# One table instead of two in a two-layer graph network on one core: all gathers of layer 1 ahead of its additions, gathered rows and messages passed through DRAM

## The chip, the cores and the metric

The kernel runs on one core of one Trainium2 chip. The metric is the device time in microseconds (us); for the kernel before it is 2267.06 us, the median of 3 runs.

## The reference, cut to what matters

```python
# x: (100000, 256) fp32; src, dst: (25000,) int32, dst sorted
deg = maximum(segment_sum(ones, dst, 100000), 1.0); deg_isqrt = deg ** -0.5
# layer 0
h = maximum(_layernorm(x), 0.0)
x = x + deg_isqrt * segment_sum((deg_isqrt * h)[dst] * edge_weight[:, None], src)
# layer 1
h = maximum(_layernorm(x), 0.0)
x_i, x_j = h[dst], h[src]
feat = concatenate([x_i, x_j - x_i])              # (25000, 512)
msg = relu(feat @ W1 + b1) @ W2 + b2              # W1 (512, 512), W2 (512, 256)
x = x + segment_sum(msg, dst) / (segment_sum(ones, dst) + 1e-8)
```

Only rows that are an end of an edge change; the rest of the 100,000 rows (102.4 MB) is copied. Layer 1 must read every row as layer 0 left it, before layer 1 adds anything to it.

## The kernel before, in words

The edges are padded to 200 tiles of 128, in NB = 50 batches of W = 4 tiles. A batch of layer 0 needs four gathers (indirect DMAs of 128 rows of 1 KB) and four scatters (indirect DMAs that add 128 rows into the table). A batch of layer 1 needs eight gathers, for both ends of each edge, and four scatters. All gathers and scatters are issued by GpSimd (POOL) and all go through one software queue.

The prep stage and layer 0 copy `x` into a DRAM table `x1_d` (400 pieces of 250 KB on SyncE's queue, eight in flight), and layer 0 adds into `x1_d`. A barrier ends layer 0. Layer 1 gathers from `x1_d`, while SyncE copies the whole of `x1_d` into `out`, again 400 pieces (L889, L894). The scatters of layer 1 go to `out` and may start only when this second copy is done. POOL's program in layer 1 is written out: first the gathers of LEAD1 = 20 batches (L907), where a batch waits until the batch two before it has been normalized, since `ends` has two buffers; then the wait for the copy; then 100 groups, each of two scatters (L919), three of the remaining gathers while there are any, and a wait until the two scatters have landed. The sums to be scattered lie in `e_ring`, a ring of 20 batches in SBUF.

The other engines run one software-pipelined step per batch. TensorE (PE): `mlp_in` (48 matmuls of 512 columns, `ps_h`), `sums` of the batch before (16 matmuls into `ps_s`, L1240), and twice `turn` (transposes of `e_normed`, `ps_t`) and `mlp_out` (24 matmuls each, `ps_m`). ScalarE (ACT): `std_of`, `hid_high`, `norm` of the next batch (`ends` to `e_normed`), `feat_high`, `scale` of the batch before (`ps_s` to `e_ring`), `out_high`, and the load of `dst_row` for two batches on. VectorE (DVE): the low parts, the comparison tables, and `moments_of` for two batches on.

## Time and profile before

| | us |
|---|---|
| median of 3 runs (2262.39 to 2270.36) | 2267.06 |
| the profiled execution, its own time | 2282.08 |
| its span | 2280.2 |
| layer 1 in it, from the first gather | 1007.4 to 2280.2 |
| POOL busy, PE busy (whole span) | 1280.2, 1762.0 |

The profiled execution is 15.0 us above the median. POOL's busy time leaves out about 0.3 us between two of its DMA instructions, and PE's busy time is modelled from pipelined matmuls, so both are read beside the times at which things start.

### The profile page before, as it was taken

What the parts mean: (1) busy time and instruction counts of PE and PEld (TensorE: products, weight loads), DVE (VectorE), ACT (ScalarE), POOL (GpSimd) and SP (SyncE); (2) the same over time, 40 slices, a digit from 0 to 9 for tenths busy, and PEclk for the clock granted to TensorE, in tenths of its full rate; (3) what the DMA queues carried; (4) which work ended last, traced back from release to release, by engine and by line L of the source; (5) the groups of instructions that cost most, each with busy time, mean ns of one, the idle gap of its engine ahead of it and who ended that gap; (6) DMA issues with size and microseconds to landing.
All of it is one profiled execution on the core that took longest, in us unless ns stands there. A gap on an engine that the chain in (4) does not pass through costs nothing.

```text
span 2280.2 us, 46975 instructions
## 1 busy us (share of the span) xinstructions
PE 1762.0 (77%) x14020; PEld 1536.3 (67%) x14020; DVE 1500.0 (66%) x6001; ACT 1033.7 (45%) x2106; POOL 1280.2 (56%) x1024
## 2 busy tenths in 40 slices
PE   7958888776665667207888888999999999999960
PEld 2258778776665657206777777788888888888850
DVE  8979888886666667205555555667777777777730
ACT  0025454443333333105544554566666666666630
POOL 2032222478888888653332222248888888888754
PEclk9989899998888778658998888999999999999985
DMA  8999999466666666458999999225555555555533
GB/s 297 316 297 338 310 338 311 116 109 101 104 103 104 103 103 104 56 140 279 309 299 295 297 295 292 64 65 94 91 95 97 93 96 99 94 92 97 88 44 39
DMA packets 142793, 379.71 MB, mean 167 GB/s; under 512 B 31805, under 2 KB 97352, under 8 KB 129864
## 3 DMA queue, kind: packets, MB, share of 16 engines
q0 software_dynamic: 86400, 131.14, 32.5%
q1 hardware_dynamic: 27452, 208.63, 26.6%
q10 hardware_dynamic: 28912, 39.64, 6.7%
q14 instruction: 20, 0.16, 0.0%
q8 instruction: 9, 0.15, 0.0%
HBM read 325.72 MB, written 259.17 MB: 257 GB/s over the span
## 4 chain that ended last, share of the span: by engine, by line
PE 24%; issue 11%; POOL 10%; ACT 5%; DMA 3%; DVE 2%; another core or an unknown queue 1%; ACTq 0%; DVEq 0%; POOLq 0%
PE ps_h L1213 12%; PE ps_m L1227 7%; POOL table_out L919 5%; POOL ends L907 5%; PE ps_t L1200 2%; ACT e_normed L1111 2%; DMA table_out<-e_ring,e_targets_all 2%; PE ps_s L1240 2%; ACT hid L1125 1%; DMA ends<-x,keys 1%; DVE e_moments L960 1%; ACT feat_hi L1118 1%; ACT e_ring L1143 0%; DVE out_sum L1032 0%
## 5 line engine op out<-in xcount | busy, mean ns | idle before, releaser
L907 POOL DMA_INDIRECT ends<-x,keys x400 | 402.1, 1005 | 437.4 <-ACT e_normed L1111 312.9
L768 PE MATMUL ps_deg<-table,hot 128*128 128x128 bf16 x5600 | 358.1, 225 | 82.9 <-issue 69.4
L768 PEld LDWEIGHTS ps_deg<-table,hot 128*128 128x128 bf16 x5600 | 334.5, 101 | 101.8 <-issue 92.2
L919 POOL DMA_INDIRECT table_out<-e_ring,e_targets_all x200 | 326.6, 1633 | 108.0 <-issue 54.8
L461 POOL DMA_INDIRECT x<-sums_ring,targets_all x200 | 329.6, 1648 | 89.3 <-issue 65.8
L451 POOL DMA_INDIRECT rows<-in_x,row_idx x200 | 207.4, 1037 | 252.2 <-ACT normed L695 198.2
L1213 PE MATMUL ps_h<-feat_hi,w_hi 128*128 128x512 f32 x800 | 321.3, 402 | 8.9 <-ACT hid L1125 6.5
L1213 PE MATMUL ps_h<-feat_lo,w_hi 128*128 128x512 f32 x800 | 318.8, 399 | 0.5 <-issue 0.5
L1213 PE MATMUL ps_h<-feat_hi,w_lo 128*128 128x512 f32 x800 | 318.2, 398 | 0.7 <-issue 0.7
L782 PE MATMUL ps_sum<-msg_hi,same 128*128 128x260 f32 x800 | 153.3, 321 | 158.8 <-issue 151.7
L1227 PE MATMUL ps_m<-w_hi,hid_hi 128*128 128x256 f32 x800 | 243.1, 304 | 15.6 <-issue 8.3
L1227 PE MATMUL ps_m<-w_lo,hid_hi 128*128 128x256 f32 x800 | 233.7, 292 | 13.4 <-issue 13.4
L1027 DVE TENSOR_TENSOR feat_lo<-ps_t,feat_hi 128x512 fp32r<-128x512 f32 x200 | 130.8, 687 | 165.7 <-ACT feat_hi L1118 87.2
L782 PEld LDWEIGHTS ps_sum<-msg_hi,same 128*128 128x128 f32 x800 | 129.4, 223 | 163.9 <-issue 163.9
L1227 PE MATMUL ps_m<-w_hi,hid_lo 128*128 128x256 f32 x800 | 234.3, 293 | 6.0 <-issue 5.9
L1022 DVE TENSOR_TENSOR hid_lo<-hid,hid_hi 128x512 fp32r<-128x512 f32 x200 | 138.6, 693 | 123.6 <-ACT hid_hi L1128 97.3
L1200 PE MATMUL ps_t<-ident,e_normed 128*128 128x128 f32 x800 | 113.0, 284 | 133.2 <-ACT e_normed L1111 92.5
L1111 ACT ACTIVATE e_normed<-ends,e_shift,e_rstd 128x256 f32<-128x256 f32 x400 | 211.1, 587 | 0.5 <-issue 0.5
L1132 ACT ACTIVATE out_hi<-out_sum 128x512 fp32r<-128x512 f32 x100 | 63.2, 632 | 317.5 <-DVE out_sum L1032 265.0
L1213 PEld LDWEIGHTS ps_h<-feat_hi,w_hi 128*128 128x128 f32 x800 | 151.9, 190 | 52.5 <-ACT hid L1125 10.8
L1200 PEld LDWEIGHTS ps_t<-ident,e_normed 128*128 128x128 f32 x800 | 93.1, 146 | 139.2 <-ACT e_normed L1111 93.1
L513 DVE TENSOR_SCALAR hot<-hi_row,hi_ident 128x1024 bf16<-128x1024 f16 x350 | 147.4, 492 | 49.2 <-issue 21.1
(140 smaller groups left out, 3593.6 us busy)
## 6 DMA issues: line engine op xcount, KB each, us to landing
table_out<-x SPq DMA_DIRECT2D x400, 252.0 KB
x<-in_x SPq DMA_DIRECT2D x400, 250.0 KB
hi_row<-hi_rows ACTq DMA_DIRECT2D x50, 256.0 KB
src_row<-src_rows ACTq DMA_DIRECT2D x50, 256.0 KB
dst_row<-dst_rows ACTq DMA_DIRECT2D x50, 256.0 KB
ends<-x,keys POOLq DMA_INDIRECT x400
rows<-in_x,row_idx POOLq DMA_INDIRECT x200
x<-sums_ring,targets_all POOLq DMA_INDIRECT x200
```

What stands on the lines that cost most here:

```text
L451: pool.indirect_dma_start(out=rows[b % 2][:, j, :], out_offset=None, in_=x, in_offset=bass.IndirectOffsetOnAxis(ap=row_idx[:, W * b + j:W ...
L461: pool.indirect_dma_start(out=x1_d, out_offset=bass.IndirectOffsetOnAxis(ap=targets_all[:, b, j:j + 1], axis=0), in_=sums_ring[:, b % RING ...
L513: last = nc.vector.tensor_scalar(hot[:, c, :, :], hi_row[q][:], hi_ident[:, c:c + 1], None, ALU.is_equal)
L768: last = nc.tensor.matmul(ps_deg[q][k][:, j * P:(j + 1) * P], hot[:, c, k, j * P:(j + 1) * P], table[:, c, part, :], start=(c == 0 and par ...
L782: nc.tensor.matmul(ps_sum[a][:, 0:CW], same[:, j, a * P:(a + 1) * P], msg_hi[:, j, :], start=(j == 0), stop=False)
L907: pool.indirect_dma_start(out=ends[b % 2][:, n, :], out_offset=None, in_=x1_d, in_offset=bass.IndirectOffsetOnAxis(ap=keys[:, 1 - end, at: ...
L919: pool.indirect_dma_start(out=out, out_offset=bass.IndirectOffsetOnAxis(ap=e_targets_all[:, b, j:j + 1], axis=0), in_=e_ring[:, b % RING1, ...
L1022: nc.vector.tensor_tensor(hid_lo[:, m, :], hid[m % 2][:], hid_hi[:, m, :].bitcast(fp32), ALU.subtract).then_inc(hid_lo_done, 1)
L1111: last = nc.scalar.activation(e_normed[:, r, :], ends[q][:, r, :], ACT.Relu, bias=e_shift[q][:, r:r + 1], scale=e_rstd[q][:, r:r + 1])
L1200: last = nc.tensor.transpose(ps_t[k % 2][:, j * P:(j + 1) * P], e_normed[:, end * W + j, c * P:(c + 1) * P], ident[:])
L1213: last = nc.tensor.matmul(ps_h[m % 2][:], w[:, k, m * P:(m + 1) * P], f[:, k, :], start=(k == 0 and n == 0), stop=(k == KF - 1 and n == 2))
L1227: last = nc.tensor.matmul(ps_m[g][:, a * D:(a + 1) * D], h[:, m, at:at + P], w[:, m, :], start=(m == 0 and n == 0), stop=(m == KH - 1 and ...
```

## The change

`x1_d` is gone. `x` is copied once, into `out`; layer 0 adds into `out`, layer 1 gathers from `out` and adds into `out`. For that, all 400 gathers of layer 1 stand ahead of its 200 scatters. Since neither the gathered rows nor the sums of all batches fit in SBUF, they pass through two DRAM tensors:

- Batches 0 and 1 are gathered into `ends`. From batch 2 on a gather goes into `stage_rows[b % 2]`; SyncE writes each half (four gathers, 512 KB) to `ends_d` (`spilled`), and ACT loads two halves back into `ends` at the start of its step, for two batches on (`load_ends`).
- `norm` writes in place, into `ends`, and `e_normed` is gone.
- `scale` writes `e_sums[q]`, ACT stores the batch (512 KB) to `sums_d` at the end of the next step (`keep`), and SyncE loads it back into a quarter of the `stage_rows` buffers (`back`, four batches deep) once all spills are done. POOL scatters from there, with the same wait after each group of two scatters.
- Tiles used by layer 0 alone are given free before layer 1. `dst_f`, a copy of the edge targets as fp32, replaces `per_edge` there.
- DW = 2 equals G = 2, so the matmuls of `sums`, `peers` and `after` are the same in number and shape as before.

```diff
-            out_flat = out...; x1_d = nc.dram_tensor("x1", (ROWS, D), fp32).ap()
+    ends_d = nc.dram_tensor("ends_d", (NB, P, 2 * W * D), fp32).ap()
+    sums_d = nc.dram_tensor("sums_d", (NB, P, W * D), fp32).ap()
...
             @block.sync
             def _(sp):
-                for k in range(FLIGHT):
-                    sp.dma_start(out_flat[k], x1_flat[k]).then_inc(bulk_out[k], 16)
-                with sp.Fori(1, ROUNDS) as r:
-                    for k in range(FLIGHT):
-
-                        sp.wait_ge(bulk_out[k], 16 * r)
-                        sp.dma_start(out_flat[bass.ds(FLIGHT * r + k, 1)],
-                                     x1_flat[bass.ds(FLIGHT * r + k, 1)]).then_inc(bulk_out[k], 16)
+                with sp.Fori(0, HALF - 1) as t:
+                    for q in range(2):
+                        for end in range(2):
+                            sp.wait_ge(staged[q][end], 16 * W * (t + 1))
+                            sp.dma_start(ends_d[...], stage_rows[q][...]).then_inc(spilled[q][end], 16)
+                for q in range(2):
+                    for end in range(2):
+                        sp.wait_ge(spilled[q][end], 16 * (HALF - 1))
+                for b in range(NB):
+                    sp.wait_ge(kept[b % 2], 16 * (b // 2 + 1))
+                    if b >= BACK:
+                        sp.wait_ge(back_free, b - BACK + 1)
+                    sp.dma_start(back(b)..., sums_d[b, :, :]).then_inc(back_in[b % BACK], 16)
...
                 def gather(b, n):
-                    if n == 0 and b >= 2:
-                        pool.wait_ge(e_normed_done, b + 1)
+                    if b >= 4 and j == 0:
+                        pool.wait_ge(spilled[b % 2][end], 16 * (b // 2 - 1))
...
-                for b in range(LEAD1):
+                for b in range(NB):
                     for n in range(2 * W):
                         gather(b, n)
-                for k in range(FLIGHT):
-                    pool.wait_ge(bulk_out[k], 16 * ROUNDS)
-                left = 2 * W * (NB - LEAD1)
-                for c in range(GROUPS * NB):
-                    scatter(c // GROUPS, c % GROUPS)
-                    for n in range(min(left, 3 * c), min(left, 3 * (c + 1))):
-                        gather(LEAD1 + n // (2 * W), n % (2 * W))
-                    scatter_end(c // GROUPS, c % GROUPS)
+                for q in range(2):
+                    pool.wait_ge(ends_first[q], 16 * 2 * W)
+                    for end in range(2):
+                        pool.wait_ge(spilled[q][end], 16 * (HALF - 1))
+                for b in range(NB):
+                    for g in range(GROUPS):
+                        scatter(b, g)
+                        scatter_end(b, g)
...
+                def load_ends(b, t, q):
+                    act.wait_ge(turned, KF * (b - 1))
+                    for end in range(2):
+                        act.wait_ge(spilled[q][end], 16 * t)
+                        act.dma_start(ends[q][:, end * W:(end + 1) * W, :]..., ends_d[...]).then_inc(ends_in[q], 16)
+                def keep(b, q):
+                    act.wait_ge(e_scaled, GROUPS * (b + 2))
+                    act.dma_start(sums_d[...], e_sums[q][:]...).then_inc(kept[q], 16)
```

On POOL's queue, where the lead of gathers ended before, a group of layer 1 was two scatters into `table_out` (the tensor `out`) and up to three gathers:

```order
L907 DMA ends<-x,keys 128x256 [waits e_normed_done]
L907 DMA ends<-x,keys 128x256 x7
L919 DMA table_out<-e_ring,e_targets_all 100800x256 [waits bulk_out5,bulk_out6,bulk_out4,bulk_out7,bulk_out3,e_in_ring,bulk_out2,e_target_ready,bulk_out1,bulk_out0]
L919 DMA table_out<-e_ring,e_targets_all 100800x256
L907 DMA ends<-x,keys 128x256 [waits e_normed_done]
L907 DMA ends<-x,keys 128x256 x2
L919 DMA table_out<-e_ring,e_targets_all 100800x256 [waits e_in_ring,e_scattered]
L919 DMA table_out<-e_ring,e_targets_all 100800x256
L907 DMA ends<-x,keys 128x256 x3
```

On the same queue, the last gathers of batch 49 and the first scatters after the change:

```order
L932 DMA stage_rows<-table_out,keys 128x256 [waits spilled10]
L932 DMA stage_rows<-table_out,keys 128x256 x3
L932 DMA stage_rows<-table_out,keys 128x256 [waits spilled11]
L932 DMA stage_rows<-table_out,keys 128x256 x3
L943 DMA table_out<-stage_rows,e_targets_all 100800x256 [waits spilled10,spilled11,ends_first1,back_in0,spilled01,e_target_ready,spilled00,ends_first0]
L943 DMA table_out<-stage_rows,e_targets_all 100800x256
L943 DMA table_out<-stage_rows,e_targets_all 100800x256 [waits e_scattered]
L943 DMA table_out<-stage_rows,e_targets_all 100800x256
L943 DMA table_out<-stage_rows,e_targets_all 100800x256 [waits e_scattered,e_target_ready,back_in1]
```

No gather stands between a group's scatters and the wait for them any more, and the gathers wait for spills, not for `e_normed_done`.

On ACT's queue, from the last `out_hi` of a step to the first `hid` of the next, before the change:

```order
L1132 ACTIVATE out_hi<-out_sum 128x512 [waits b2_added]
L1092 REGISTER_ALU
L1093 ISA [waits dst_row_free]
L1093 DMA dst_row<-dst_rows 128x512
L1101 ACTIVATE e_std<-e_mean_var,eps_col 128x8 [waits e_rstd_done,e_var_done]
L1124 REGISTER_ALU [waits mm1_done]
L1125 ACTIVATE hid<-ps_h,b_col 128x512 [waits hid_lo_done]
```

The same place after it:

```order
L1173 ACTIVATE out_hi<-out_sum 128x512 [waits b2_added]
L1178 DMA sums_d<-e_sums 128x1024 [waits e_scaled]
L1128 DMA dst_row<-dst_rows 128x512 [waits dst_row_free]
L1136 DMA ends<-ends_d 128x1024 [waits spilled00,turned]
L1136 DMA ends<-ends_d 128x1024 [waits spilled01]
L1145 ACTIVATE e_std<-e_mean_var,eps_col 128x8 [waits e_rstd_done,e_var_done]
L1166 ACTIVATE hid<-ps_h,b_col 128x512 [waits hid_lo_done,mm1_done]
```

One DMA issue has become four, all of them ahead of `e_std` and `hid`.

## Rows read from the trace of the kernel before

**Rows 1.** Source line L919, all scatters of layer 1: duration min/median/max ns, first and last start.

```profile
L919 POOL DMA_INDIRECT table_out<-e_ring,e_targets_all x200: 1552/1622/2093, 1502.1 to 2271.3; - x100
```

**Rows 2.** Timeline of POOL at the very end: start, duration, idle before.

```profile
2263.49 1.55 POOL L919 DMA_INDIRECT table_out<-e_ring,e_targets_all  x1 [3.06 <-DMA table_out<-e_ring,e_targets_all]
2265.34 1.55 POOL L919 DMA_INDIRECT table_out<-e_ring,e_targets_all  x1 [0.30 <-issue]
2269.41 1.55 POOL L919 DMA_INDIRECT table_out<-e_ring,e_targets_all  x1 [2.52 <-DMA table_out<-e_ring,e_targets_all]
2271.27 1.55 POOL L919 DMA_INDIRECT table_out<-e_ring,e_targets_all  x1 [0.30 <-issue]
```

**Rows 3.** Timeline of POOL, one group of two scatters and three gathers.

```profile
1572.42 1.68 POOL L919 DMA_INDIRECT table_out<-e_ring,e_targets_all  x1 [0.30 <-issue]
...
1580.72 1.62 POOL L919 DMA_INDIRECT table_out<-e_ring,e_targets_all  x1 [0.30 <-issue]
```

**Rows 4.** Timeline of POOL during the second copy, the first two gathers of a batch.

```profile
1300.20 0.94 POOL L907 DMA_INDIRECT ends<-x,keys  x1 [17.70 <-ACT e_normed L1111]
1301.45 0.95 POOL L907 DMA_INDIRECT ends<-x,keys  x1 [0.30 <-issue]
```

**Rows 5.** Source line L907, window 1000:1500, what POOL waited for: us, times.

```profile
L907 POOL DMA_INDIRECT ends<-x,keys x159: 940/946/1407, 1007.4 to 1499.6; - x159
  ACT e_normed L1111: 297.2, 18
```

**Rows 6.** Source line L1240 on PE, windows 1075:1440, 1430:1530 and 1550:2165.

```profile
L1240 PE MATMUL ps_s<-out_hi,peers x104: 278/280/281, 1078.6 to 1413.8; 128*128 128x256 f32 x104
...
L1240 PE MATMUL ps_s<-out_hi,peers x32: 278/280/281, 1442.9 to 1518.7; 128*128 128x256 f32 x32
...
L1240 PE MATMUL ps_s<-out_hi,peers x232: 278/280/281, 1558.7 to 2150.4; 128*128 128x256 f32 x116
```

**Rows 7.** Windows: length, busy PE PEld DVE ACT POOL, PEclk, DMA share, GB/s.

```profile
1444.00:1454.00 10.00, 8.01 (x65) 7.58 (x64) 3.29 (x7) 2.25 (x5) 6.62 (x7) 1.00 0.36 105
1560.00:2150.00 590.00, 579.72 (x3585) 510.38 (x3584) 433.01 (x1425) 387.56 (x755) 476.37 (x374) 1.00 0.52 95
2206.00:2275.00 69.00, 0.00 (x0) 0.00 (x0) 0.00 (x0) 0.00 (x0) 34.16 (x22) 0.50 0.39 43
1020.00:1420.00 400.00, 322.64 (x1760) 281.38 (x1760) 215.34 (x728) 198.34 (x378) 119.21 (x125) 0.87 0.91 296
```

**Rows 8.** DMA queues of the whole span: packets, MB, share of 16 engines.

```profile
q0 software_dynamic: 86400, 131.14, 32.5%
q1 hardware_dynamic: 27452, 208.63, 26.6%
q10 hardware_dynamic: 28912, 39.64, 6.7%
```

**Rows 9.** Timeline of the SyncE queue at the start of the second copy.

```profile
1006.62 5.10 SPq L889 DMA_DIRECT2D table_out<-x  x8
...
1012.14 12.78 SPq L894 DMA_DIRECT2D table_out<-x  x8
```

**Rows 10.** Chain that ended last, window 950:1035, landing of batch 0's last gather.

```profile
1016.31 7.96 DMA ends<-x,keys
```

**Rows 11.** Timeline of POOL in layer 0: a batch's last scatter, and the next scatter.

```profile
880.50 1.55 POOL L461 DMA_INDIRECT x<-sums_ring,targets_all  x1 [0.30 <-issue]
...
885.14 1.62 POOL L461 DMA_INDIRECT x<-sums_ring,targets_all  x1 [0.47 <-issue]
```

**Rows 12.** Timeline of ACT: at a step's boundary, and before a step's last `hid`.

```profile
1719.31 0.34 ACTq L1093 DMA_DIRECT2D dst_row<-dst_rows  x1
1720.39 0.67 ACT L1125 ACTIVATE hid<-ps_h,b_col 128x512 f32<-128x512 f32 x1
...
1328.35 0.69 ACT L1125 ACTIVATE hid<-ps_h,b_col 128x512 f32<-128x512 f32 x1 [0.46 <-PE ps_h L1213]
```

**Rows 13.** Timeline of PE during the second copy, a pause inside one step.

```profile
1311.98 1.11 PE L1200 MATMUL ps_t<-ident,e_normed 128*128 128x128 f32 x4 [4.03 <-issue]
```

More of the change, by code:

```diff
@@ L814, in gnn_preln_two_layers @@
             e_shift = [sb(f"e_shift{q}", [P, 2 * W], fp32) for q in range(2)]
-            e_normed = sb("e_normed", [P, 2 * W, D], fp32)
+            stage_rows = [sb(f"stage_rows{q}", [P, 2 * W, D], fp32) for q in range(2)]
             feat_hi = sb("feat_hi", [P, KF, W * P], fp32r)
@@ L841, in gnn_preln_two_layers @@
             ps_s = [pb(f"ps_s{h}", [P, G * D], fp32) for h in range(2)]
+            ends_first = [sem(f"ends_first{q}") for q in range(2)]
             ends_in = [sem(f"ends_in{q}") for q in range(2)]
+            staged = [[sem(f"staged{q}{end}") for end in range(2)] for q in range(2)]
+            spilled = [[sem(f"spilled{q}{end}") for end in range(2)] for q in range(2)]
             dst_row_in = [sem(f"dst_row_in{q}") for q in range(2)]
@@ L871, in gnn_preln_two_layers @@
             e_summed = sem("e_summed")
-            e_in_ring = sem("e_in_ring")
-            e_ring_free = sem("e_ring_free")
+            e_scaled = sem("e_scaled")
+            kept = [sem(f"kept{q}") for q in range(2)]
+            back_in = [sem(f"back_in{k}") for k in range(BACK)]
+            back_free = sem("back_free")
             e_scattered = sem("e_scattered")
@@ L877, in gnn_preln_two_layers, with back @@
             block = stage.enter_context(nc.Block())
+            def back(b):
+                k = b % BACK
+                return stage_rows[k // 2][:, k % 2 * W:(k % 2 + 1) * W, :]
             def following(b, t, q):
@@ L947, in _ @@
                 dve.sem_inc(dst_row_free, 2)
+                nc.vector.tensor_copy(dst_f[:], keys[:, 1, :].rearrange("p (b j) -> p b j", j=W))
                 nc.vector.memset(after[:], 0.0).then_inc(after_made, 1)
                 dve.wait_ge(after_made, 1)
-                nc.vector.memset(after[:, 0, P:G * P], 1.0)
-                nc.vector.tensor_copy(after[:, 0, 0:P], later[:])
-                nc.vector.tensor_copy(after[:, 1, P:G * P], later[:]).then_inc(after_made, 1)
+                for a in range(DW):
+                    if a + 1 < DW:
+                        nc.vector.memset(after[:, a, (a + 1) * P:DW * P], 1.0)
+                    last = nc.vector.tensor_copy(after[:, a, a * P:(a + 1) * P], later[:])
+                last.then_inc(after_made, 1)
                 dve.wait_ge(after_made, 2)
                 def moments_of(b, t, q, part):
-                    if part == 0:
-                        dve.wait_ge(ends_in[q], 16 * 2 * W * (t + 1))
+                    if part == 0 and isinstance(b, int) and b < 2:
+                        dve.wait_ge(ends_first[q], 16 * 2 * W)
+                    elif part == 0:
+                        dve.wait_ge(ends_in[q], 32 * t)
                     for r in range(part * W, (part + 1) * W):
@@ L1054, in step @@
                         feat_low(b + 1, 1)
-                    if second:
+                    if second and not first(b):
                         moments_of(b + 2, t + 1, q, 0)
@@ L1061, in step @@
                     out_low(b, 0)
-                    if second:
+                    if second and not first(b):
                         moments_of(b + 2, t + 1, q, 1)
                     add_b2(b, 1)
-                    if second:
+                    if second and not first(b):
                         mean_var_of(b + 2, t + 1, q)
                     out_low(b, 1)
+                    if second and first(b):
+                        moments_of(b + 2, t + 1, q, 0)
+                        moments_of(b + 2, t + 1, q, 1)
+                        mean_var_of(b + 2, t + 1, q)
                 for b in range(2):
@@ L1106, in norm @@
                         act.wait_ge(e_shift_done, b + 1)
-                        if not first(b):
-                            act.wait_ge(turned, KF * b)
                     for r in range(r0, r1):
-                        last = nc.scalar.activation(e_normed[:, r, :], ends[q][:, r, :], ACT.Relu,
+                        last = nc.scalar.activation(ends[q][:, r, :], ends[q][:, r, :], ACT.Relu,
                                                     bias=e_shift[q][:, r:r + 1], scale=e_rstd[q][:, r:r + 1])
@@ L1165, in step @@
                         if not first(b):
-                            scale(b - 1, 1 - q, g)
+                            scale(b - 1, t - 1 + q, 1 - q, g)
                         out_high(b, g)
+                    if load and first(b):
+                        load_ends(b + 2, t + 1, q)
+                    if not first(b):
+                        keep(b - 1, 1 - q)
                     if load:
@@ L1184, in _ @@
                 for g in range(GROUPS):
-                    scale(NB - 1, 1, g)
+                    scale(NB - 1, HALF - 1, 1, g)
+                keep(NB - 1, 1)
             @block.tensor
@@ L1200, in turn @@
                         last = nc.tensor.transpose(ps_t[k % 2][:, j * P:(j + 1) * P],
-                                                   e_normed[:, end * W + j, c * P:(c + 1) * P], ident[:])
+                                                   ends[q][:, end * W + j, c * P:(c + 1) * P], ident[:])
                     last.then_inc(turned, 1)
```

131 lines of the change are left out of this document (73 added, 58 removed).

## The prediction, made before the changed kernel ran

> **What bounds the kernel now.** I read the source line of the layer 1 scatters first. Its last instruction starts at 2271.3 us and the span ends at 2280.2 [rows 1], so POOL's chain sets the end. Layer 1 occupies POOL from 1007.4 [rows 5], and it splits in three. In the lead (1007.4 to 1502.1 [rows 1, 5]) POOL is not the limit: it issues a gather every 1.25 us (1300.20 to 1301.45 [rows 4]), so its 159 gathers need 199 us, and it waits 297.2 us, 18 times, for `e_normed` [rows 5]. It is PE that paces the lead: from the first start of `ps_s` to the last, less 1.6 us inside one step, 13 steps take (1413.8 - 1.6 - 1078.6) / 12 = 27.8 us each [rows 6]. In the second part a group of two scatters and three gathers takes 1580.72 - 1572.42 = 8.3 us [rows 3], and POOL hardly waits: busy 476.37 of 590 us [rows 7], the rest mostly the 0.30 us between instructions. PE steps take (2150.4 - 1.6 - 1558.7) / 28 = 21.1 us there [rows 6]. In the third part only scatters are left: a group pair takes 2269.41 - 2263.49 = 5.92 and, by the idle times 2.5 and 3.1 that alternate, 6.5 us [rows 2], so about 6.25 per group. As a check: the 240 gathers left make 80 groups with gathers and 20 without, and (2271.3 - 1502.1 - 20 x 6.25) / 80 = 8.05 [rows 1]. The wait in it is for the landing of its own second scatter. PE has two steps and its last `sums` to go at 2150.4 [rows 6], so it is done near 2200 and POOL trails it by some 80 us at the end.
>
> The second copy holds layer 1 in two ways: no scatter may start before it ends, and while it runs the DMA share is 0.91 [rows 7] and PE pauses inside its steps, as the 4.03 us ahead of four transposes that wait for nothing the trace shows [rows 13]. Between the end of the copy and the mixed part, with bursts of gathers but no copy, a step still takes (1518.7 - 1.6 - 1442.9) / 3 = 24.7 us [rows 6].
>
> **The change part by part, POOL's chain.** Prep and layer 0 keep their instructions; only the name of the table they add into changes. I cost that at nothing, so the first gather starts at 1007.4.
>
> *Gathers.* 400 at 1.25 us are 500 us, 10.0 per batch, if nothing holds them. What can hold them is the spill. A half of `stage_rows` is four gathers; the next gather into it starts 13 gathers, 16.25 us, after the half's last gather was issued. In that time the gather must land (3.8 to 8.0 us: below, the scatter pair's landing, 5.92 - 1.85 = 4.1 less waking [rows 2]; above, the first batch under the copy [rows 10]), SyncE must issue (0.64 us, 5.10 / 8 [rows 9]), and 512 KB must land in DRAM. The trace has no such store; the nearest row is the first 250 KB piece of the copy, waited for at 1012.14 and issued from 1006.62, so 5.5 us [rows 9]; I take 5 to 8. The sum is 9.5 to 16.7 us: usually inside 16.25, so 10.0 per batch is the lower bound and a little more is likely.
>
> *The DMA engines.* Eight gathers in 10 us alone have share 0.36 [rows 7], 0.45 us of all 16 engines each. One scatter has 0.39 x 69 / 22 = 1.22 us [rows 7]. For 512 KB on a hardware queue: 208.63 MB took 0.266 x 2280 = 606 us, so 1.5 us; by q10 (39.64 MB, 6.7%) 2.0 us [rows 8]; I take 1.7. The gather phase then needs per 10 us 3.6 + 2 x 1.7 = 7.0 us, and per 21 us PE step two loads, one `keep` and a `dst_row`, 3 x 1.7 + 1.0 = 6.1. That is 0.70 + 0.29 = 0.99, or 0.91 by 1.5 us. It is near full. Against a collapse speaks that under the copy, with share 0.91, POOL still issued at 1.25 us [rows 4]. I take 10.3 us per batch.
>
> *Turnover.* After the last gather (landing, spill, first `back`) I add 15 us: 4 + 5.5 + 5.5.
>
> *Scatters.* 100 groups with nothing between the second scatter and the wait: 6.25 us each alone, 12.5 per batch. New beside them are the loads, `keep` and `back`, 2.8 transfers of 512 KB per 12.5 us, a share of about 0.4 beside scatter's own 0.4. The trace prices this once: in layer 0, with 0.5 MB per batch of other loads (a share of about 0.1), a batch's last scatter had landed 885.14 - 880.50 = 4.6 us after its start [rows 11]; this is one of 18 such places between 480 and 900 us, which range from 4.6 to 5.6 with mean 4.95, against 1.55 + 3.06 = 4.6 with nothing beside it [rows 2]; 0.25 to 0.3 us for 0.1 of share. Scaled to 0.3 to 0.4 of share this is 0.6 to 1.0 us per group, less since `back` is issued just after a landing and falls in the first scatter's shadow. I take 13.7 per batch. Bounds: 12.5 (all hidden), and 12.5 + 2.8 x 1.7 = 17.3 (none hidden).
>
> The Trainium skill, "DMA: Bandwidth & Descriptors", section "Issuing engines are not separate DMA queues", says that DMAs of all issuing engines run on the same 16 DMA engines and interleave. This speaks against the change: by it none of the new traffic is free. If each queue had engines of its own the scatters would keep 12.5 us per batch and the sum below would be 60 us less; the 4.95 against 4.6 us above agrees with the page.
>
> *Sum.* 1007.4 + 50 x 10.3 + 15 + 50 x 13.7 = 2222, and 4.5 us from the last wait to the end of the span (8.9 [rows 1] less the 4.4 that the last group's period holds): a span of 2227, own time 2229.
>
> **PE's chain, which must not be longer.** The first `ps_s` stays at about 1078.6. Until 1537 the gather bursts go on; I take the 24.7 us of the stretch with bursts and no copy (bounds 21.1 and 27.8 [rows 6]): 19 steps, to 1548. After that 29 steps at 21.1 + 0.6. The 0.6 is ACT: three more DMA issues of 0.34 us and their address registers, some 1.5 us, ahead of `hid`, which starts 1.1 us after the `dst_row` issue now [rows 12]. Its cover is ACT's idle time before the last `hid`, 0.46 us [rows 12], and about 0.4 us between `hid_lo` and `mlp_out`; without cover it is 1.5. That gives 2177, and 11 us for the last step, 2188. The tail is new: `scale` 2, store 5, load 5, two groups 6.25 + 7 = 25 us. PE's chain ends at 2213, 14 us before POOL's. In-place `norm`, `dst_f` and the smaller tiles are costed at nothing: same shapes, on DVE and ACT under PE's 21 us. The wait of `load_ends` for `turned` and `spilled` ahead of `e_std` and `hid` on ACT is long met: the spills run at 10 us per batch against PE's 21 or more; only at batch 2 may a few us be lost, and the first landing without the copy (4 instead of 8 us) gives them back.
>
> The profiled execution lies 15 us above the median, so **the median should be 2229 - 15 = 2214 us**.
>
> **The rivals.**
> 1. *All transfers hide.* 10.0 and 12.5 us per batch: 1007.4 + 500 + 15 + 625 + 4.5 = 2152, median 2139. For it: small packets, and POOL kept its pace under a busier copy. Against: the 4.95 against 4.6 us. Chance 0.15.
> 2. *PE is the bound.* Its pauses under DMA load stay as under the copy, 27.8 us for 16 steps (to 1523), and ACT's 1.3 us come in full, 32 steps of 22.4: 2240, and 11 + 25: 2276, median 2262, level with before; with 21.7 us steps 2240. For it: the share in the gather phase is as high as under the copy. Against: pieces of 4 KB, not 16 KB, and no wait that explains the pauses. Chance 0.13.
> 3. *Slower: the DMA queues hold POOL.* The mechanism is the landing of spills, then of scatters. The point from which it decides: (2280.2 - 1007.4 - 15 - 4.5) / 50 = 25.1 us for the two together, against my 24.0, so only 1.1 us per batch away. Spills that land after 19 instead of 16 us make 11.5 per batch (two batches share the excess), and a `back` or load behind each second scatter 15.0: 26.5, span 2352, median 2336. For it: the share of 0.99 and the bound of 17.3. Chance 0.18.
> That removing the copy does nothing is excluded: POOL's 297 us of waits in the lead [rows 5] hang on it.
>
> **How the numbers follow.** My forecast has 0.54, its own range 2180 to 2255. With rival 1 below and part of rivals 2 and 3 above, 8 in 10 lie between 2140 and 2300. Under 0.3% (7 us) a change cannot be told from none: faster is below 2260. Faster: 0.54 + 0.15 + half of rival 2, 0.75; same 0.07; slower 0.18.
>
> **What would show it.** The last gather of layer 1 should start near 1520, with short waits for the SyncE spill at every fourth gather; the first scatter near 1537; groups of 6.6 to 7.0 us, with waits of 3 to 4 us for their own landing; PE steps of 24 to 25 us before 1540 and 21.5 to 22 after; POOL's last scatter some 10 to 15 us later than PE's own chain would give. The prediction is wrong if a gather batch takes over 11 us or under 10, if groups take over 7.5 us, or if POOL waits for `back` (PE bound) over a long stretch.

## The result

The changed kernel takes 2630.91 us (median of 4, 2629.06 to 2632.29) beside 2268.71 us for the kernel before: ratio 1.159, interval 1.1543 to 1.1637. The forecast was 2214 us, faster, with a range of 2140 to 2300: the sign is wrong, and the range ends 330 us below the result.

Each set of runs was made in one session on a chip, and the sessions came in two kinds: in one ("held") the kernel before takes 2264 to 2277 us and the changed one 2630, in the other ("free") 2152 to 2162 and 2283. The result above, and the trace ahead of the prediction, are from held sessions.

The page's slices of the changed kernel, and its costliest groups:

```profile
PE   7788878766656611111102139999999999999994
DVE  9888889776766711000000027777777777777772
POOL 2132234888888856777777723332333232233333
PEclk9899999888887856555555559999999999999997
DMA  8999995665656544666666635555555555555554
...
L943 POOL DMA_INDIRECT table_out<-stage_rows,e_targets_all x200 | 326.1, 1630 | 760.4 <-DMA stage_rows<-sums_d 533.5
L932 POOL DMA_INDIRECT stage_rows<-table_out,keys x384 | 392.0, 1021 | 121.4 <-issue 121.4
```

Each digit is 66 us. While POOL gathers (from the sixteenth digit to the twenty-fourth), PE is mostly at 0 to 2 tenths; before, PE was busy for 0.81 of the lead (322.64 of 400 [rows 7]). Only after the gathers does PE run, and then it is full to the end, so POOL's scatters wait 533.5 us for `back`, that is for PE. The source lines of POOL date it (gathers, then scatters):

```profile
L932 POOL DMA_INDIRECT stage_rows<-table_out,keys x384: 945/950/1929, 1020.9 to 1532.8; - x192
L932 POOL DMA_INDIRECT ends<-table_out,keys x16: 945/949/1023, 1000.7 to 1019.6; - x16
  issue: 125.9, 399
...
L943 POOL DMA_INDIRECT table_out<-stage_rows,e_targets_all x200: 1552/1567/2068, 1577.7 to 2618.8; - x100
  DMA stage_rows<-sums_d: 533.5, 46
  DMA table_out<-stage_rows,e_targets_all: 128.6, 51
  DVE e_targets_all L1049: 65.6, 3
```

POOL did what was forecast: 400 gathers from 1000.7 to 1532.8 us, 10.66 us per batch, and no wait for the spill. PE did not. Its `ps_s` line, windows 1010:1560 and 1560:2627:

```profile
L1298 PE MATMUL ps_s<-out_hi,peers x8: 275/326/418, 1425.1 to 1438.0; 128*128 128x256 f32 x8
...
L1298 PE MATMUL ps_s<-out_hi,peers x392: 274/282/387, 1576.4 to 2593.1; 128*128 128x256 f32 x196
```

These rows set against [rows 6] are the whole result. Eight matmuls of this form are one batch. Before, 13 batches were done by 1413.8 us. Now one is done by 1560, and the other 49 begin at 1576.4. All but the last follow each other at the usual pace: the last batch's come 11 us behind the one before, so (2593.1 - 11 - 1576.4) / 47 = 21.4 us is a step, and 1576 + 47 x 21.4 = 2582, with 45 us of last step and tail, is the span of 2627. What PE does meanwhile is this (timeline of PE, then of POOL, at 1200 us):

```profile
1202.09 0.37 PE L1283 MATMUL ps_m<-w_lo,hid_hi 128*128 128x256 f32 x1 [1.73 <-issue]
1204.88 0.37 PE L1283 MATMUL ps_m<-w_hi,hid_lo 128*128 128x256 f32 x1 [2.43 <-issue]
1207.68 0.37 PE L1283 MATMUL ps_m<-w_hi,hid_hi 128*128 128x256 f32 x1 [2.43 <-issue]
1210.48 0.37 PE L1283 MATMUL ps_m<-w_lo,hid_hi 128*128 128x256 f32 x1 [2.43 <-issue]
...
1200.97 0.95 POOL L932 DMA_INDIRECT stage_rows<-table_out,keys  x1 [0.30 <-issue]
1202.22 0.95 POOL L932 DMA_INDIRECT stage_rows<-table_out,keys  x1 [0.30 <-issue]
```

One matmul starts every 2.80 us and waits for nothing that the trace names ("issue"). ACT sees the same beat (timeline of ACT): each of the four slices of `hid` needs 12 matmuls, and 12 x 2.80 = 33.6 us lie between two of them, while ACT's own instructions keep their length.

```profile
1071.91 0.69 ACT L1166 ACTIVATE hid<-ps_h,b_col 128x512 f32<-128x512 f32 x1 [32.13 <-issue]
...
1105.50 0.69 ACT L1166 ACTIVATE hid<-ps_h,b_col 128x512 f32<-128x512 f32 x1 [30.77 <-remote]
...
1139.10 0.69 ACT L1166 ACTIVATE hid<-ps_h,b_col 128x512 f32<-128x512 f32 x1 [30.77 <-remote]
```

The two views agree in the total and not in the detail. PE's own records of the 12 matmuls ahead of the middle one stand close together (timeline of PE, first and last of the 12, then the next slice):

```profile
1072.65 0.80 PE L1269 MATMUL ps_h<-feat_hi,w_hi 128*128 128x512 f32 x1 [27.23 <-ACT hid L1166]
...
1077.45 0.40 PE L1269 MATMUL ps_h<-feat_hi,w_lo 128*128 128x512 f32 x1
1106.24 0.80 PE L1269 MATMUL ps_h<-feat_hi,w_hi 128*128 128x512 f32 x1 [28.39 <-ACT hid L1166]
```

By these records the slice is done near 1078, yet ACT, which waits for it, starts at 1105.50. The profile models the ends of matmuls, so for the 512-column matmuls the 2.80 us is worked out from ACT's rows. Over the whole gather phase it is 500 us for 215 matmuls, 2.3 us each.

PE's granted clock falls to the 1.2 GHz level in this stretch (0.5 in the slices), after PE has stood mostly idle: a 256-column matmul then takes 0.37 us, and that explains nothing of the 2.8.

Loading of code is not it either, as far as the trace records it: in the window 1200:1350 PE has 48 matmuls, and these two are all the DMA queues that moved anything, neither of the kind "instruction":

```profile
q0 software_dynamic: 5301, 14.48, 37.9%
q1 hardware_dynamic: 4132, 15.03, 26.8%
```

### The profile page after: what moved, and what is told of

Same layout as the page of the kernel before. It is cut to its first block, busy times and chain, and to the rows that moved or that the text cites. A ratio compares the mean times of both kernels' runs of the same rounds, so it can differ in the third digit from the quotient of the medians.

```text
span 2627.3 us, 45849 instructions
## 1 busy us (share of the span) xinstructions
PE 1776.8 (68%) x14020; PEld 1532.8 (58%) x14020; DVE 1493.3 (57%) x6002; ACT 1028.4 (39%) x2106; POOL 1286.3 (49%) x1024
## 3 DMA queue, kind: packets, MB, share of 16 engines
q10 hardware_dynamic: 49936, 116.19, 14.9%
## 4 chain that ended last, share of the span: by engine, by line
another core or an unknown queue 16%; ACT 15%; issue 10%; DVE 8%; PE 8%; ACTq 3%; DMA 1%; POOL 1%; DVEq 0%; POOLq 0%
ACT ends L1152 8%; PE ps_m L1283 6%; ACT hid L1166 4%; DVE out_sum L1063 2%; DVE e_moments L991 2%; ACTq L1136 2%; DVE feat_lo L1058 1%; ACT hid_hi L1169 1%; PE ps_h L1269 1%; DVE hid_lo L1053 1%; ACT feat_hi L1159 1%; DVE out_lo L1068 1%; ACTq L1178 1%; ACTq L1128 1%
## 5 line engine op out<-in xcount | busy, mean ns | idle before, releaser
L943 POOL DMA_INDIRECT table_out<-stage_rows,e_targets_all x200 | 326.1, 1630 | 760.4 <-DMA stage_rows<-sums_d 533.5
L932 POOL DMA_INDIRECT stage_rows<-table_out,keys x384 | 392.0, 1021 | 121.4 <-issue 121.4
L1269 PE MATMUL ps_h<-feat_hi,w_hi 128*128 128x512 f32 x800 | 328.2, 410 | 169.2 <-ACT hid L1166 142.7
L464 POOL DMA_INDIRECT table_out<-sums_ring,targets_all x200 | 330.8, 1654 | 87.9 <-issue 63.9
L1283 PE MATMUL ps_m<-w_hi,hid_hi 128*128 128x256 f32 x800 | 236.5, 296 | 106.9 <-DVE hid_lo L1053 72.2
L1283 PE MATMUL ps_m<-w_hi,hid_lo 128*128 128x256 f32 x800 | 227.3, 284 | 32.4 <-issue 32.2
L1166 ACT ACTIVATE hid<-ps_h,b_col 128x512 f32<-128x512 f32 x200 | 133.9, 670 | 245.9 <-remote 207.7
L1256 PE MATMUL ps_t<-ident,ends 128*128 128x128 f32 x800 | 110.5, 282 | 173.5 <-ACT ends L1152 85.7
L1283 PEld LDWEIGHTS ps_m<-w_hi,hid_hi 128*128 128x128 f32 x800 | 154.3, 193 | 119.8 <-DVE hid_lo L1053 84.4
L1152 ACT ACTIVATE ends<-ends,e_shift,e_rstd 128x256 f32<-128x256 f32 x400 | 211.1, 588 | 0.5 <-DVE e_shift L1006 0.5
```

The costliest lines, as they stand in the source:

```text
L464: pool.indirect_dma_start(out=out, out_offset=bass.IndirectOffsetOnAxis(ap=targets_all[:, b, j:j + 1], axis=0), in_=sums_ring[:, b % RING0 ...
L932: pool.indirect_dma_start(out=(ends if b < 2 else stage_rows)[b % 2][:, n, :], out_offset=None, in_=out, in_offset=bass.IndirectOffsetOnAx ...
L943: pool.indirect_dma_start(out=out, out_offset=bass.IndirectOffsetOnAxis(ap=e_targets_all[:, b, j:j + 1], axis=0), in_=back(b)[:, j, :], in ...
L1152: last = nc.scalar.activation(ends[q][:, r, :], ends[q][:, r, :], ACT.Relu, bias=e_shift[q][:, r:r + 1], scale=e_rstd[q][:, r:r + 1])
L1166: nc.scalar.activation(hid[m % 2][:], ps_h[m % 2][:], ACT.Relu, bias=b1_col[:, m:m + 1])\
L1269: last = nc.tensor.matmul(ps_h[m % 2][:], w[:, k, m * P:(m + 1) * P], f[:, k, :], start=(k == 0 and n == 0), stop=(k == KF - 1 and n == 2))
```

## The experiments

At first sight three things are new beside PE in that stretch: gathers without a pause, the spills, and the loads that ACT issues. The theory was that the unbroken gathers hold PE by themselves; the rivals were the DMA traffic of spills and loads, and, for the kernel before, its second copy.

**Session 1, free** (before 2152.42 us), each kernel run once. The first kernel takes the second copy out of the kernel before; all but one of its 400 pieces are left out, so most output rows are unwritten.

```
             def _(sp):
-                for k in range(FLIGHT):
-                    sp.dma_start(out_flat[k], x1_flat[k]).then_inc(bulk_out[k], 16)
...
+                sp.dma_start(out_flat[0], x1_flat[0]).then_inc(bulk_out[0], 16)
```

> The kernel before, with one piece of the second copy in place of 400 (it leaves the rest of the output rows unwritten; everything else as before). Theory B (bursts): PE is held by streams of gathers that POOL issues without a pause, whatever else the DMA engines do; then a PE step of the lead, with its burst of 8 gathers, stays at 25 us or more (27.8 with the copy), and the whole is 2220 to 2275 us. Theory S (share): PE is held because the DMA engines are full (share 0.91 under the copy); then a lead step falls to about 21.1 us, POOL's first scatter comes near 1385, and the whole is 2150 to 2175 us.

Measured: 2151.88 us. Its lead steps are 20.4 to 20.5 us with 8 gathers in a burst. It equals the kernel before of its session, which was itself 116 us faster than in the result. So the question could not be tested there. PE was not held in this kernel, and by its time not in the kernel before either (no trace of that one from a free session was kept).

The second kernel lets POOL wait, in the changed kernel, for the landing of every 4 gathers.

```
                         .then_inc(ends_first[b] if b < 2 else staged[b % 2][end], 16)
+                    if j == W - 1 and b >= 2:
+                        pool.wait_ge(staged[b % 2][end], 16 * W * (b // 2))
```

> The changed kernel, in which POOL waits after every 4 gathers until they have landed (from batch 2 on). Theory B: pauses of about 4 us free PE, so PE steps in the gather phase take 21 to 27 us instead of about 190; a batch of gathers takes about 18 us, the last starts near 1900, and POOL's 100 groups at 6.25 follow: 2540 to 2600 us in all. Theory S: the share falls from 0.65 to about 0.4, with the same result; only if neither holds does PE stay frozen and the whole exceed 2900 us.

Measured: 2544.03 us. POOL waits 356.9 us, 95 times, and PE's steps during the gathers are 21.1 to 22.1 us.

The third keeps the gathers but drops the spills: ACT loads rows of `x` in place of the gathered rows, so layer 1 computes on other data.

```
-                            sp.wait_ge(staged[q][end], 16 * W * (t + 1))
-                            sp.dma_start(ends_d[bass.ds(2 * t + 2 + q, 1), :, end * W * D:(end + 1) * W * D]
...
-                                      ends_d[bass.ds(b, 1), :, end * W * D:(end + 1) * W * D]
+                                      x_chunks[bass.ds(b, 1), :, end * W * D:(end + 1) * W * D]
```

> The changed kernel without the spills: SyncE writes nothing to ends_d, POOL waits for the landing two batches back instead, and ACT loads its rows from x (so layer 1 computes on other rows; sizes, counts and places of all other work are unchanged). Theory B: the gathers alone freeze PE; PE matmuls of the gather phase still start about 2.8 us apart, the gather phase takes about 500 us, and the whole is 2580 to 2630 us. Theory S: with a third or so of the traffic gone (share under 0.5) PE steps of the gather phase fall to 21 to 25 us and the whole to 2150 to 2230 us.

Measured: 2276.59 us, between the two ranges expected, with PE's steps 21.4 us and POOL waiting 346.8 us for the landing of its own scatters. I could have read this as proof that the spills hold PE. It was not: the changed kernel itself takes 2283 in such a session.

The fourth spaces the gathers with an iota of 1024 columns.

```
+                    if b >= 2:
+                        pool.wait_ge(padded_n, 2 * W * (b - 2) + n)
+                        nc.gpsimd.iota(pad_i[:], [[1, PADW]], base=0, channel_multiplier=0).then_inc(padded_n, 1)
```

> The changed kernel with a POOL instruction of about 1.2 us (an iota into a scratch tile) after every gather from batch 2 on; POOL stays busy and waits for no landing, gathers come every 2.6 to 2.8 us. Theory B in its strict form (only a pause for landings frees PE): PE stays frozen for some 1050 us, the whole is over 3000 us. Theory R (the rate of gathers decides, 0.8 per us holds PE and 0.37 per us, as in the mixed part of the kernel before, does not): PE steps of 21 to 27 us in the gather phase, and the whole is about 2700 us, set by POOL.

Measured: 2559.43 us where about 2700 was expected, since a gather came every 2.2 us and not every 2.6 to 2.8; PE steps of 23 to 28 us during the gathers, 21.5 after.

**Session 2, held** (before 2269.26 us), runs repeated: both kernels unchanged.

> The changed kernel as it is. The kernel before took 2152.4 us on the chip of the first experiments and 2268.7 us where the change was timed, so both need a trace from one chip. If the freeze of PE under the gathers belongs to the changed program: about 2630 us again. If it belongs to the chip or the placement of that execution: PE steps of 21 to 27 us in the gather phase, and 2150 to 2280 us.

> The kernel before as it is, on the same chip. Where it takes about 2152 us its PE steps under the second copy should be 20.5 to 22 us and its chain at the end POOL's or PE's alike; where it takes about 2268 us they should be 27.8 us.

Measured: 2631.47 us, ratio 1.1598 (1.1574 to 1.1621), and 2271.44 us, ratio 1.0011 (0.9989 to 1.0034). The result repeats, with the idle PE and the lead steps of 27 to 31 us.

**Session 3, free** (before 2159.98 us), on another chip, each kernel run once: three kernels of session 1 again, and the changed kernel beside them.

> The changed kernel as it is, as the yardstick of this group, since the two groups so far ran on different chips (before: 2152 on one, 2269 us on the other). Theory C (chip): where before takes about 2152 us, PE is not frozen under the gathers and this takes 2200 to 2290 us; where before takes about 2269, it takes 2630. Theory P (program: the streams of gathers together with the spills freeze PE on any chip): 2630 on either.

> The changed kernel without spills, its rows read from x (as e3). On a chip with before at 2269: theory G (the gathers alone freeze PE there) says matmuls of the gather phase about 2.8 us apart and 2600 to 2630 us; theory P says PE runs free and 2230 to 2290 us. On a chip with before at 2152: 2277 again.

> The kernel before with one piece of the second copy (as e1; most output rows stay unwritten). On a chip with before at 2269: theory G says a lead step with its burst of 8 gathers stays over 24 us, 2230 to 2269 us; theory P says 20.5 us and about 2152. On a chip with before at 2152: 2152 again.

> The changed kernel with a wait for the landing after every 4 gathers (as e2). On a chip with before at 2269: if pauses of about 4 us free PE, steps of 21 to 27 us in the gather phase and 2540 to 2560 us; if bursts of 4 already hold PE, steps over 30 us and over 2700. On a chip with before at 2152: 2544 again.

Measured: 2282.60, 2262.58, 2152.52 and 2535.04 us. The first is the most useful trace of the study, for here the changed kernel runs as forecast in kind. Its POOL source lines, and then two windows, of its gather and its scatter phase (length, busy PE PEld DVE ACT POOL, PEclk, DMA share, GB/s):

```profile
L932 POOL DMA_INDIRECT stage_rows<-table_out,keys x384: 942/946/1425, 1024.6 to 1515.9; - x192
L932 POOL DMA_INDIRECT ends<-table_out,keys x16: 942/946/1022, 1004.5 to 1023.3; - x16
...
L943 POOL DMA_INDIRECT table_out<-stage_rows,e_targets_all x200: 1552/1566/2045, 1528.6 to 2272.2; - x100
  DMA table_out<-stage_rows,e_targets_all: 365.3, 95
  DMA stage_rows<-sums_d: 11.7, 1
```

```profile
1010.00:1510.00 500.00, 455.77 (x2732) 394.96 (x2733) 337.89 (x1123) 301.38 (x587) 381.17 (x391) 0.97 0.85 276
1560.00:2100.00 540.00, 526.83 (x3226) 458.83 (x3225) 381.86 (x1275) 346.01 (x676) 218.89 (x137) 1.00 0.66 149
```

The same window of the changed kernel in the held session of the result:

```profile
1010.00:1510.00 500.00, 76.35 (x215) 54.82 (x216) 32.48 (x116) 29.27 (x53) 381.38 (x376) 0.53 0.64 199
```

POOL is equally busy in both (381 us). PE has 2732 matmuls in one and 215 in the other, and the DMA share is higher where PE runs. A full DMA is therefore not what stops PE.

**Session 4, held** (before 2263.64 us), runs repeated: no spill, and the wait after 4.

> The changed kernel without spills (as e3 and e8), wanted on a chip where before takes about 2269 us and the changed kernel 2630. Theory G (there the stream of gathers alone holds PE): matmuls of the gather phase about 2.8 us apart, 2600 to 2630 us. Theory P (gathers and spills together are needed): PE steps of 21 to 25 us, 2230 to 2290 us. On a chip of the other kind: 2263 to 2277 us as before, and nothing new.

> The changed kernel with a wait for the landing after every 4 gathers (as e2 and e10), wanted on the same kind of chip. If pauses of about 4 us free PE: steps of 21 to 27 us in the gather phase and 2535 to 2560 us, some 80 us faster than the changed kernel there. If bursts of 4 already hold PE: steps over 30 us, over 2700 us. On a chip of the other kind: 2535 to 2544 us.

Measured: 2626.32 us, ratio 1.1611 (1.1558 to 1.1664), and 2527.28, ratio 1.1173 (1.1107 to 1.1239), 8 us under the range expected. The windows of the gather phase, of the kernel without spills and then of that with the waits:

```profile
1010.00:1510.00 500.00, 73.89 (x216) 52.88 (x217) 32.47 (x116) 29.25 (x53) 381.03 (x376) 0.53 0.35 103
```

```profile
1010.00:1510.00 500.00, 464.33 (x2777) 402.31 (x2778) 338.49 (x1134) 307.10 (x597) 232.63 (x239) 0.97 0.62 202
```

Without spills the DMA share is 0.35 and PE is held all the same, 216 matmuls for 215. With a pause of 348.7 / 95 = 3.7 us after every 4 gathers PE is free, at a share of 0.62. These two runs separate the theories: the gathers hold PE, and a pause frees it. The time stays long because POOL pays for the pauses, and its last gather starts at 1826.6 us.

**Session 5, held** (before 2276.97 us), on a fourth chip, runs repeated but for the last kernel.

> The kernel before without its second copy (one piece of it is kept, so most rows of the output stay unwritten). If POOL's bursts of 8 gathers hold TensorE by themselves, the lead's steps stay at 27 to 28 us and the time at 2245 to 2270 us. If it takes the copy beside them, the steps fall to 20.5 us, as they did in the first such run, and the time to about 2152.

Measured: 2203.63 us, ratio 0.9669 (0.9627 to 0.971). Neither end of the expectation: the lead's steps are 21.7 to 24.7 us, mean (1444 - 1070) / 16 = 23.4. A burst of 8 alone costs some 3 us per step, and with the copy beside it about 7. So the copy does deepen the hold in the kernel before, which the theory in its plain form did not say.

> The changed kernel with an iota of 1024 columns after each gather of layer 1, beside kernels whose TensorE stands still under the gathers. The gathers then take until about 1876 us (2.25 us each, instead of 1.33). If what holds TensorE is how close the gathers follow each other, its steps are 23 to 27 us meanwhile and the time is that of the first run, 2550 to 2570. If it is that POOL never pauses for a landing, TensorE still stands until 1876, and 48 steps of 21.5 us and the tail give about 2950.

Measured: 2565.72 us, ratio 1.1257, last gather at 1857.5, PE steps of 23 to 27 us, as in the free session. POOL never pauses for a landing here, and PE is not held. So what counts is not the missing wait as such, but how many gathers follow each other how closely.

Nor are the 2 to 5 us by which these steps exceed 21.5 a rest of the hold: they are there in the free session too, where the changed kernel's steps are 21.4 to 22.3 but for two, and the trace gives them another cause. These are PE's costliest wait and two VectorE lines in window 1100:1500 of this run, then the same VectorE lines of the changed kernel in the free session, and last this run's window 1010:1510:

```profile
L1289 PE MATMUL ps_m<-w_hi,hid_hi 128*128 128x256 f32 x268 | 85.5, 319 | 44.3 <-DVE hid_lo L1059 44.3
L1026 DVE TENSOR_SCALAR peers<-dst_row,dst_col 128x256 fp32r<-128x256 f32 x64 | 57.3, 955 | 0.2
L1059 DVE TENSOR_TENSOR hid_lo<-hid,hid_hi 128x512 fp32r<-128x512 f32 x65 | 54.7, 841 | 13.4 <-ACT hid_hi L1175 13.4
...
L1053 DVE TENSOR_TENSOR hid_lo<-hid,hid_hi 128x512 fp32r<-128x512 f32 x72 | 49.9, 693 | 35.7 <-ACT hid_hi L1169 35.6
L1020 DVE TENSOR_SCALAR peers<-dst_row,dst_col 128x256 fp32r<-128x256 f32 x72 | 23.5, 386 | 0.5
...
1010.00:1510.00 500.00, 428.67 (x2466) 375.23 (x2467) 358.31 (x1012) 271.61 (x529) 458.25 (x457) 0.93 0.60 188
```

Beside the iotas VectorE's comparison takes 955 ns for 386 and `hid_lo` 841 for 693, and PE waits for `hid_lo`, not for "issue". POOL is busier here (458 us of 500) than in the changed kernel (381), so a busy POOL is not what holds PE.

The third kernel turns the finding to use. It is the kernel **before**, with one wait in the lead:

```
                         .then_inc(ends_in[b % 2], 16)
+                    if b < LEAD1 and n == W - 1:
+                        pool.wait_ge(ends_in[b % 2], 16 * (2 * W * (b // 2) + W))
```

> The kernel before, with POOL waiting in the lead for the landing of each batch's first 4 gathers before it issues the other 4. POOL has 297 us to spare there. If unbroken gathers hold TensorE and a pause of about 4 us frees it, some 16 steps of the lead fall from 27.8 to 21 to 22 us, and the time from 2265 to 2155 to 2180, below both kernels. If the lead's long steps come from the second copy's traffic, nothing changes: 2260 to 2275.

Measured: 2181.23 us (2180.41 to 2188.73), ratio 0.9581 (0.9548 to 0.9615). It beats both kernels in a held session. The source lines of its gathers in the lead and of `ps_s` in window 1075:1440, then its window 1010:1410:

```profile
L907 POOL DMA_INDIRECT ends<-x,keys x160: 940/946/1461, 1004.2 to 1409.8; - x160
  ACT e_normed L1113: 107.8, 17
  DMA ends<-x,keys: 102.0, 20
...
L1242 PE MATMUL ps_s<-out_hi,peers x138: 278/280/281, 1080.2 to 1439.7; 128*128 128x256 f32 x138
```

```profile
1010.00:1410.00 400.00, 359.62 (x2189) 315.29 (x2190) 267.40 (x896) 241.36 (x467) 154.53 (x156) 0.95 0.94 318
```

POOL waits 102.0 us for landings and 107.8 for `e_normed`, where it waited 297.2 [rows 5]; together that is less, because the steps it waits for fall from 27.8 to 21.1 us. The lead ends at 1409.8 instead of 1499.6 [rows 5], and those 90 us are nearly all of the gain. The second copy is still there, and moves at 318 GB/s for all traffic instead of 296 [rows 7]. So the copy, which the change removes as the culprit, deepens the hold (the first kernel of session 5), but the lead gets its short steps back with the copy in place.

> The changed kernel once more, one look with no timed rounds, in one session with timed ones. If the two levels seen so far (2630 and 2283 us) belong to the session, it is 2630 us here with the kernel before at about 2265; if they belong to looks without timed rounds, it is about 2283.

Measured: 2630.06 us. A kernel that is run only once can show the held level; the level goes with the session.

**Session 6, free** (before 2161.70 us), on the same chip as session 5, each kernel run once.

> The kernel before with the waits in the lead once more. In a session in which the kernel before takes 2150 to 2160 us, its lead steps are 20.5 us already, so the waits have nothing to give: 2150 to 2185 us. In one in which it takes about 2265, again 2175 to 2195.

> The changed kernel with a pause for the landing after every 8 gathers of layer 1 instead of every 4: 10.3 us of gathers and 3.7 us of pause, so the gathers last until about 1016 + 48 x 14 = 1690 us and POOL's scatters, 6.8 us a group, until about 2370. If a burst of 8 still holds TensorE (some 6 us in each step of the lead of the kernel before), TensorE does 14 to 20 steps by 1690 and ends at 2390 to 2450; if not, POOL decides, at 2350 to 2385.

The second of the two has the wait once per 8 gathers:

```
+                    if n == 2 * W - 1 and b >= 2:
+                        pool.wait_ge(staged[b % 2][end], 16 * W * (b // 2))
```

Measured: 2177.56 us and 2417.26 us. Where PE is not held, the waits in the lead cost 16 us (0.7%, one run of each): POOL now waits 142.3 us for landings. The 2417.26 us lie in the range that was expected of a held PE (2390 to 2450), and yet POOL sets it: its last gather starts at 1693.9, and a group of scatters takes 7.0 us where 6.8 was taken. The wait per 8 leaves PE's steps at 21.3 to 22.3 us, but in a free session that says nothing of a burst of 8 in a held one. That stays untried.

| session | chip | kernel before | changed kernel |
|---|---|---|---|
| of the result | not recorded | 2268.71 | 2630.91 |
| 1 | 2 | 2152.42 | not run |
| 2 | 1 | 2269.26 | 2631.47 |
| 3 | 12 | 2159.98 | 2282.60 |
| 4 | 2 | 2263.64 | not run |
| 5 | 7 | 2276.97 | 2630.06 |
| 6 | 7 | 2161.70 | not run |

Chips 2 and 7 appear in both kinds, so the kind is not the chip's. One thing goes with the kind throughout: in the free sessions (1, 3 and 6) every kernel was run once, and in the held ones (2, 4, 5 and the result's) kernels were run repeatedly. The fourth run of the changed kernel was a single one in a held session and was held, so the repetition of a kernel by itself does not decide; whether that of its neighbours does was not tried. What sets the kind is open. Kernels whose gathers are paused or spaced nearly agree in both: 2181.23 and 2177.56 us with the waits in the lead, 2527.28 (held) and 2544.03 and 2535.04 with the wait after 4, 2565.72 and 2559.43 with the iota.

## Why the prediction was wrong

**The step that failed is PE's chain.** "I take the 24.7 us of the stretch with bursts and no copy (bounds 21.1 and 27.8)": measured, PE does one step in the whole gather phase. Both bounds were read from a lead in which POOL gathers for 10 us and then rests for 17.7. The changed kernel's gathers have no rest, so 27.8 was no upper bound; it was the price at a duty of 10 in 27.8. The rows shown would have told it. The step was 27.8 - 21.1 = 6.7 us longer for 10 us of gathers [rows 6], so PE lost 0.67 of the time that a burst lasts. At a duty of one a step is 21.1 / 0.33 = 64 us, 7 steps fit before 1537, 41 steps of 21.7 are left, and with 11 and 25 us of last step and tail the sum is 2463: PE bound and slower, though still short of the 2627 measured. The rest would need a hold that grows with the length of the burst, which is argued below and not shown. [Rows 13] showed the pause too, 4.03 us on a PE that waits for nothing. I put it down to the second copy's load, because the copy was the other thing running. Session 5 parts the two: the copy deepens the pause, and a wait between gathers removes it with the copy in place. In the free session the same term was off the other way: the steps of the gather phase were 21.4 to 22.3 us but for two (20.8 and 23.7), where 24.7 was taken.

**The copy was not gating the scatters either.** "No scatter may start before it ends" is so in the program, but these windows of the kernel before (columns as in [rows 7]) show that the copy was over first:

```profile
1420.00:1430.00 10.00, 5.26 (x25) 4.87 (x26) 4.61 (x10) 4.09 (x9) 1.70 (x2) 0.57 0.83 272
1430.00:1440.00 10.00, 10.00 (x45) 8.42 (x45) 7.37 (x29) 6.10 (x12) 0.00 (x0) 0.91 0.08 26
```

The traffic ends near 1430, and the first scatter starts at 1502.1 [rows 1], just behind the lead's last gather at 1499.6 [rows 5]. What delayed the scatters was the lead, and so PE.

**Rival 2 had the right bound and the wrong size.** It said PE, and gave 2262 us with 27.8 us steps for 16 steps. The sign that the last section named, POOL waiting for `back` over a long stretch, is what the trace shows (533.5 us).

**POOL's chain was mostly right, and is seen in the free session.** Gathers: 10.3 us per batch forecast, (1515.9 - 1004.5) / 49.9 = 10.25 measured, with a DMA share of 0.85 where 0.99 was feared, and no wait for a spill. Turnover: 15 forecast, 1528.6 - 1515.9 = 12.7. Scatters: 13.7 per batch forecast, (2272.2 - 1528.6) / 49.75 = 14.9 measured; the term is 60 us too small. The wait for a scatter's own landing was 365.3 / 95 = 3.85 us against 3.06 and 2.52 with nothing beside it [rows 2]. I had discounted the scaled price (0.6 to 1.0 us per group) because `back` falls in the first scatter's shadow; no run shows that shadow, and the upper end, 1.0, without a discount gives 14.5, near what was measured. The Trainium skill, "DMA: Bandwidth & Descriptors", section "Issuing engines are not separate DMA queues", had the sign of this term (DMAs of all issuers share the 16 engines); the trace agrees, with 14.9 for 12.5. With 14.9 the sum 2227 becomes 2287, against 2280.7. The kernel without spills is 20 us shorter (2262.58 for 2282.60, one run of each), but its first scatter starts no earlier (1529.7 for 1528.6): the gain lies behind the last spill, where the two differ only in what ACT loads, so it prices no spill, and which of the loads, `keep` and `back` costs the 60 us stays open. The steps after the gathers were 21.4 to 22 us where 21.7 was taken. One figure of the rivals is a slip that changes nothing: a span of 2352 gives a median of 2339 by the rule used for the others, not 2336.

**Even so the change would not have gained.** In the free session POOL sets the end, as forecast, and the changed kernel is still 5.7% slower than the kernel before (2282.60 for 2159.98, one run of each). The forecast gain compared a POOL chain without pauses with a kernel before whose lead was itself held: its 18 waits for `e_normed`, 297.2 us [rows 5], came from steps of 27.8 us; in the free session they are 66.5 us in the kernel before with the waits in its lead, whose steps are 20.4 to 21.6. What the prediction hung on removing the copy was, for the most part, the hold. Taking the copy out gains 0.5 and 7.5 us in the free sessions and 73 in a held one; pausing the gathers of the lead gains 96 there with the copy in.

**What is shown and what is only argued.** Shown: unbroken gathers hold PE without the spills (session 4), a pause of 3.7 us after 4 frees it (sessions 4 and 5), a spacing of (1857.5 - 1021.0) / 383 = 2.18 us instead of 1.33 does so too, though at this spacing the iotas slow VectorE, and the kind of session decides whether any of it happens. Excluded: a full DMA, the spills, a busy POOL, and recorded loading of code. Argued: that the hold grows with the burst. Per step a burst of 4 costs 0 to 1 us, one of 8 some 3, an endless one takes over 90% of PE's work (215 matmuls for 2732 in the same 500 us); something that fills while gathers are in flight and drains in a pause would do this. That is a guess: no view names it, and no run measured it. Open, too, is why the copy adds 4 us per step, and what makes a session held.

## What to carry to other kernels

An interference price read from a trace belongs to the duty at which it was read: divide it by the time of the disturbing work, and scale it to the duty after the change, before calling it a bound. Before merging bursts of indirect gathers into one long run, look for matmuls that start at an even spacing and wait for nothing; where they are there, a wait for a landing after every 4 gathers, on a POOL that has slack, is a two-line change that gained 4.2% in a held session here, and cost 0.7% (one run) in a free one. And run the kernel before in more than one session before believing that what its trace shows is the kernel's.

## What the runs showed of the hardware

- In held sessions, under gathers issued every 1.25 to 1.33 us without a pause, TensorE starts one matmul of 256 columns per 2.80 us, and by ScalarE's rows one of 512 columns takes as long (three slices of `hid` 33.6 us apart for 12 matmuls), while `hid` on ScalarE (0.69 us) and `hid_lo` on VectorE (693 ns) keep their durations. The DMA share was 0.64, or 0.35 without the spills.
- Pausing the gathers after every 4, or spacing them 2.18 us apart, frees TensorE in the same kind of session: 2777 and 2466 matmuls in 500 us, for 215.
- Beside iotas of 1024 columns on GpSimd, VectorE's comparison of 256 columns took 955 ns for 386, and `hid_lo` 841 for 693.
- The same kernel on the same chip shows this in one session and not in the next: 2152.42 and 2263.64 us were both measured for the kernel before on chip 2, and 2276.97 and 2161.70 on chip 7. For the changed kernel the two levels are 2630 and 2283.
- The granted clock followed: 0.53 in the held window, 0.97 in the free one, for the same program.
